# The scale of an expert's second weights is computed eleven products later, and its halves with it

## What is computed

```
x = x + attention(layernorm(x), ctx)              # 8192 tokens of 512
t = layernorm(x)
weights = softmax of the top 2 of 8 router values
for each expert e: its 1024 tokens, by weight     # tokens = t[index[e]]
    inter = relu(tokens @ first_linear[e].T)      # 1024 x 512 by 512 x 1024
    out   = inter @ second_linear[e].T            # 1024 x 1024 by 1024 x 512
    final[index[e]] += out * weight
x = x + final
```

## Time and profile before

| | us |
|---|---|
| median of three runs | 1452.41 |
| lowest, highest | 1451.22, 1456.0 |
| profiled execution | 1458.68 |
| its span | 1456.9 |
| TensorE busy in the span | 1294.9 (89%) |
| VectorE busy | 1108.0 (76%) |
| ScalarE busy | 890.5 (61%) |
| GpSimd busy | 887.2 (61%) |

### The profile page before, as it was taken

One profiled execution on the slowest core, in us unless ns is written; L12 is line 12 of the kernel. 1 busy time (PEld: TensorE's weight loads), 2 busy tenths in 40 slices (PEclk: granted clock), 3 DMA queues, 4 the chain that ended last, 5 costly groups with the idle time before them and its releaser, 6 DMA issues. The chain is left out here.

```text
span 1456.9 us, 30729 instructions
## 1 busy us (share of the span) xinstructions
PE 1294.9 (89%) x12099; PEld 763.3 (52%) x12162; DVE 1108.0 (76%) x1969; ACT 890.5 (61%) x1405; POOL 887.2 (61%) x893
## 2 busy tenths in 40 slices
PE   7659999989998999987659989899898999989996
PEld 3436777767775767764445434344343444434442
DVE  8779898989887887889756757778686777958641
ACT  4668888878997999986554426263462726446320
POOL 3478878787876788886123754647465454846412
PEclk9969999999998999998869989999999999999998
DMA  6158999869886688878234665658376664946401
GB/s 194 53 117 212 214 252 212 216 191 202 206 212 163 170 177 199 207 172 209 91 118 147 138 190 137 189 138 215 112 167 203 143 184 128 209 144 145 124 29 58
DMA packets 362585, 239.91 MB, mean 165 GB/s; under 512 B 296313, under 2 KB 296697, under 8 KB 362442
## 3 DMA queue, kind: packets, MB, share of 16 engines
q1 hardware_dynamic: 347082, 187.29, 52.8%
q0 software_dynamic: 15360, 50.66, 11.3%
HBM read 118.98 MB, written 50.86 MB: 117 GB/s over the span
## 5 line engine op out<-in xcount | busy, mean ns | idle before, releaser
L1405 PE MATMUL ps<-w2s,hT 128*128 128x512 f16 x1536 | 333.3, 379 | 3.1 <-DVE ys L2011 3.0
L1385 PE MATMUL ps<-xS,wq 128*128 128x512 f16 x1176 | 274.9, 396 | 39.1 <-ACT running L962 34.7
L1405 PEld LDWEIGHTS ps<-w2s,hT 128*128 128x128 f16 x1536 | 150.1, 98 | 185.1 <-DVE ys L2011 4.6
L1385 PEld LDWEIGHTS ps<-xS,wq 128*128 128x128 f16 x1176 | 117.5, 101 | 195.4 <-ACT running L962 39.1
L1187 PE MATMUL ps<-xnT,wqh 128*128 128x256 f16 x1536 | 197.2, 280 | 6.4 <-ACT partq L827 6.3
L1257 PE MATMUL ps<-woh,oT 128*128 128x512 f16 x768 | 181.2, 385 | 10.7 <-POOL oT L605 4.8
L625 POOL TENSOR_TENSOR ph<-sd,ph 128x1232 f16<-128x1232 f32 x64 | 162.3, 2535 | 18.4 <-ACT ph L850 17.6
L1187 PEld LDWEIGHTS ps<-xnT,wqh 128*128 128x128 f16 x1536 | 152.9, 101 | 30.6 <-issue 5.5
L619 POOL TENSOR_TENSOR sd<-sd,rr 128x1232 f32<-128x1232 f32 x64 | 144.0, 2250 | 5.3
L688 POOL DMA_INDIRECT out_dram<-ys,idx x64 | 80.9, 1265 | 103.5 <-DVE ys L2011 85.5
L962 ACT COPY running<-ps 128x512 f32<-128x512 f32 x84 | 48.4, 584 | 133.5 <-PE ps L1385 114.7
(11 more groups left out here) (228 smaller groups left out, 2542.8 us busy)
## 6 DMA issues: line engine op xcount, KB each, us to landing
xr<-x SPq DMA_DIRECT2D x64, 256.0 KB, 3.6
xrow_dram<-x SPq DMA_DIRECT2D x64, 256.0 KB, 3.7
out_dram<-x SPq DMA_DIRECT2D x64, 256.0 KB, 4.0
stage<-w1T SPq DMA_DIRECT2D x8, 2048.0 KB, 11.5
stage<-w2T SPq DMA_DIRECT2D x8, 2048.0 KB, 9.3
xt<-x SPq DMA_DIRECT2D x59, 256.0 KB, 3.4
xs<-x SPq DMA_DIRECT2D x56, 256.0 KB
wqf<-wq SPq DMA_DIRECT2D x1, 1024.0 KB, 7.8
```

The costliest lines, as they stand in the source:

```text
L1385: ins = pe.matmul(bank[:, :], left_s[p][:, a, c, j * P:(j + 1) * P], xS[:, right_s[p][b] + c, :], start=(fresh and c == 0 and i == 0), sto ...
L1405: ins = pe.matmul(yb[z][:, :], hT[:, a, k, s * P:(s + 1) * P], w2s[:, b, k, :], start=(k == 0 and i == 0), stop=(k == 7 and i == 2))
```

## The change

The names below have (p, j) of the product in whose place of the list a step stands.

- `weight_scale(e, 2)` and `gate_scale(e)` move on VectorE from the second product, (2, 0), to the thirteenth, (1, 2).
- ScalarE's four `w_hi(e, 2, k)` move from (6, 0), (6, 1), (6, 2), (6, 3) to (6, 2), (7, 2), (6, 3), (7, 3), each behind the copy of that product.
- VectorE's four `w_lo(e, 2, k)` move from (7, 0), (7, 1), (7, 2), (7, 3) to (4, 1), (1, 3), (4, 2), (4, 3).
- The single steps of the next W1's maximum move from (6, 1), (1, 2), (6, 2), (1, 3) to (6, 1), (1, 2), (3, 1), (6, 2).
- `raw_lo(e + 1, 0)` moves from (4, 3) behind the last `sum_lo`.
- `ffn2(e, 0)` waits for W2's low halves quarter by quarter, in place of all four at its start.

```diff
+STARTED = ((6, 2), (7, 2), (6, 3), (7, 3))
+HALVED = ((4, 1), (1, 3), (4, 2), (4, 3))
...
-                    if p == 6:
-                        w_hi(e, 2, j)
+                    if (p, j) in STARTED:
+                        w_hi(e, 2, STARTED.index((p, j)))
...
-                if s == 0:
-                    pe.wait_ge(S["w2lo"], 4 * (e + 1))
...
                 for k in range(8):
+                    if s == 0 and k % 2 == 0:
+                        pe.wait_ge(S["w2lo"], 4 * e + k // 2 + 1)
...
-                    if n == 1:
+                    if (p, j) == (1, 2):
                         weight_scale(e, 2)
                         gate_scale(e)
-                    if (p, j) in ((6, 1), (1, 2), (6, 2), (1, 3)):
+                    if (p, j) in ((6, 1), (1, 2), (3, 1), (6, 2)):
                         steps(weights, 1)
                     if (p, j) == (6, 3):
                         steps(weights, 9)
-                    if e + 1 < E and (p, j) == (4, 3):
-                        raw_lo(e + 1, 0)
-                    if p == 7:
-                        w_lo(e, 2, j)
+                    if (p, j) in HALVED:
+                        w_lo(e, 2, HALVED.index((p, j)))
                 sum_lo(e, 12, 3)
+                if e + 1 < E:
+                    raw_lo(e + 1, 0)
```

## The result

The changed kernel takes 1422.03 us (median of five runs, 1419.47 to 1422.85). The kernel before took 1455.34 in five runs (1451.22 to 1456.87). The ratio is 0.9774, with a 95% interval of 0.9755 to 0.9794: 33 us less, 30 to 36. Forecast were 1415.3 us and 37 us less.

A forecast was written before the change was run, and what follows sets the result against it. TensorE was taken as the bound, with 57.7 us in seven product phases beyond the matmuls. Phases of 275.8 for 312.9 save 37.1, taking the median 1452.41 to 1415.3 us; range for 8 in 10: 1403 to 1431.

The forecast's parts named there:

- Part 1: W2's scale on VectorE at product (1, 2): no wait there, stall before (6, 1) and slow clock after it gone.
- The price of the slow clock: After the idle time before product (6, 1): clock at 0.50, 1.9 us lost to slow matmuls in expert 3.
- Part 2: Before product (1, 3): new TensorE stall of 1.5 us in experts 1 to 6, 1.05 in expert 7.
- Part 3: End of the phase, before product (3, 3): stall of 0.35 us in place of 0.24; waits by quarters cost nothing.
- Part 4: Into the next phase: W2's next load issued 1.8 us later, all passed on to y7; 3.5 us in all.
- y7: VectorE's last output row of the expert before, standing before its first sum; forecast 1.8 us later.
- the middle of two ends: Wait before the sixth product: nothing in expert 2, 1.3 us in 6; 0.7 taken for each of five.
- The rival in which the row sums stretch: GpSimd's row sums 1.0 us longer each, y7 2.3 later: 15 us in all, 1430; chance 0.10.
- Sum: Seven product phases: expert 1 43.0, experts 2 to 6 195.0, expert 7 37.85; 275.8 us for 312.9, 37.1 less.
- expert 1's slow clock: In expert 1's phase, after its own wait of 2.79 us before the sixth product: 1.9 us, staying.

The follow-up runs named there:

- The first experiment: The changed kernel with VectorE's W2 scale and gate_scale back at the second product; 1457.44 us, ratio to the kernel before 1.0012.
- the early maximum: The changed kernel with the maximum of the second expert's W1 taken in steps, earlier in expert 0; 1416.42 us, ratio to the kernel before 0.9702.
- three and with four edits together: The changed kernel with the early maximum, W2's first low half later, maxima at old products: 1400.88 us; with W2's load behind two transposes as well: 1400.31 us.

## Why the prediction was right, point by point

- **Part 1, the scale at P12.** Right. No wait for the all-reduce, no wait before P7, the clock at 1.00 in experts 2 to 7, VectorE at P12's place at +17.0 as forecast. The first experiment shows that the scale's place decides: put back, the whole gain is lost.
- **The price of the slow clock** (1.9 us in expert 3). Right in kind: with the gap filled by matmuls it doesn't occur. What it cost in the phases is less plain than the sum had it, since part of the slow time covered a wait before P10 (6.4 us gained in five phases where 12 were expected).
- **Part 2, the new wait before P19.** Expected 1.5 and 1.05, measured 1.40 and 0.94. The low half was expected to end at +26.2 and ended at 1032.40 - 1005.69 = 26.7, with 0.43 of wait before P5 in it: 26.3. Both causes were told apart by the run with the maxima at their old products: VectorE's queue in experts 1 to 6, ScalarE's chain in 7. The stall doesn't slow the clock. Two slips stand in this part: the terms for expert 7 add up to +25.65, a stall of 0.95 and not 1.05; and the stretch of before holds one low half of W2 as well, so that only a maximum and the scale are new in it. Neither moves the forecast by more than 0.1 us.
- **Part 3, the phase's end.** Expected 0.35, measured 0.24 as before (0.42 in expert 5). The second layer follows each phase with 192 matmuls in 41.60 us, so the waits by quarters cost nothing; no run shows what they are worth.
- **Part 4, y7.** Expected 1.8 us later and at +3.5 to +5.2; measured 1.7 later on average, at +3.46 to +5.22. For a single expert it was no forecast: the shift is 0.45 us in one and 2.9 in another, and in the two traces of the kernel before y7 differs by up to 0.8 in one expert. The waits before P5 are 2.0 us in all and not 3.5: the middle of two ends was too high, and P5 waits from +4.1 on (y7 at +4.53 gave 0.43, +5.22 gave 1.13) and not from +3.8. The mechanism, the load with the transposes behind it, is shown by the two runs that shift the load either way. The rival in which the row sums stretch fell: the first group of four takes 3.5 us in expert 3, where it took 3.9.
- **Sum.** Phases of 275.8 expected, 275.0 measured; 37.1 less expected, 37.9 measured. That it is this close is partly luck. The waits and expert 1's slow clock came to 18.1 us where 20.7 had been put down, and all the rest to 256.9 where 7 times 36.45 is 255.2; the two misses have opposite signs.

**What was off** is the step from the profiled execution to the median. The forecast of 1415.3 took the difference off 1452.41, the median of three runs. Of the 6.7 us by which it is low, 2.9 are that the kernel before has a median of 1455.3 in five runs. The other 3.8 are that the medians lie 33.3 us apart, where 37.1 was forecast and the two profiled executions show 37.6: the one before was 3.3 us above its kernel's median and the one after 0.9 below. The second trace of the kernel before has phases of 311.2, which makes 36.2, just past the edge of the interval of the ratio (30 to 36). The start of the second stage moves by up to 5 us between traces of this case, so a difference of two traces is no better than that; whether the rest is this or something else that the traces don't show stays open.

## What to carry to other kernels

A wait costs whatever is queued behind it on its engine: before moving a step that waits, list what stands behind it, and after moving it, add up what its new neighbours delay; here that sum, from durations of single instructions, gave the new wait to 0.1 us. Here, once the long wait was gone, the next ones were short and alike in most rounds of the loop, and the one before P19 went by moving one instruction past the one that somebody waits for; where the one before P5 was removed by itself, waits before P21 took its place, and none did once P19's was gone too. Of the parts of this change two cost time (the places of the maxima and of W2's first low half), so a change of six parts is worth taking apart. Where a matmul engine idles long enough for its clock to fall, the idle time read off the trace understates the price; but the slow matmuls may cover a shorter wait, and then not all of it comes back.

## What the runs showed of the hardware

- **The clock after an idle gap.** In the kernel before, gaps of 3.7 to 5.7 us before P7 (experts 1 to 6) and of 2.5 (expert 7) were each followed by matmuls at the granted clock of 0.50, in the changed kernel gaps of 0.9 to 1.4 us before P19 by none. With 16 unused matmuls in the gap the clock stayed at 1.00, at the same DMA load. Between these lengths both happened. Before P5, with the maxima back (expert 1) and with raw_lo back (expert 5):

```profile
846.61 19.99 PE L1387 MATMUL ps<-xS,wq 128*128 128x512 f16 x84 [2.15 <-ACT running L964]
...
1178.42 18.30 PE L1387 MATMUL ps<-xS,wq 128*128 128x512 f16 x84 [2.53 <-ACT running L964]
```

  After the shorter gap the clock fell to 0.50 from 848 on, after the longer it stayed at 1.00. What tells the two apart no run shows. The Trainium skill (TensorE: Matmul & The Clock Gate, "HAM oscillation") says that a wait between blocks of matmuls makes the next block start at the low clock; the gaps from 3.7 us on agree.
- **A transpose queued behind a load.** Two transposes took 8.67, 6.89 and 10.19 us behind a 2 MB load of W2, and 3.66 in front of it. Behind it both were through 10.4 to 10.9 us after the load was issued, whether they themselves were issued 0.5, 2.2 or 3.5 us after it.
- **GpSimd after a change of routine.** Between its last scatter and the all-reduce of W2's maximum lie 5.8 to 6.6 us, in the kernel before and after the change, and in each of the seven experts anew. In expert 3 of the kernel before two instructions named MODIFY_POOL_CONFIG stand at 1022.4, right behind the scatter, and the all-reduce starts 6.3 us after them. The Trainium skill (GPSIMD Engine Reference, "Instruction dispatch") gives about 6 us for the first call of a newly loaded routine, counted from that instruction; the trace agrees.
- **ScalarE's standstill.** Before its copy of P18 ScalarE mostly stands for 0.55 us. It stood for 3.1 to 4.5 us in experts 2, 4, 5 and 6 with W2's load behind the transposes, for 2.0 to 2.5 in experts 2 to 6 with raw_lo back, for 2.0 to 3.9 in five experts with the early maximum, and for 1.92 in expert 6 of the changed kernel itself, with nothing open that the trace shows. With three and with four edits together it didn't come. Its cause isn't settled.
